# Dense neighbour sums: every fp32 product as three bf16 products

## The reference

```python
def _fa_layer(h, row, col, Wt_l, bt_l, Wg_l, bg_l):
    h = h @ Wt_l.T + bt_l
    deg = jnp.clip(jax.ops.segment_sum(ones, row, num_segments=n), 1.0)
    dinv = deg ** (-0.5)
    g = jnp.tanh(h[row] @ Wg_l + bg_l)
    norm = g * dinv[row] * dinv[col]
    msg = norm[:, None] * h[row]
    out = jax.ops.segment_sum(msg, col, num_segments=n)
    return out + h
```

## Time and profile before

| what | value |
|---|---|
| median of 3 runs | 3548.09 us (3545.02 to 3555.73) |
| profiled execution, its own time | 3552.29 us |
| its span | 3550.4 us |
| instructions in the profile | 56998 |
| PE busy | 2215.2 us, 62% |
| DVE busy | 2218.8 us, 62% |
| POOL busy | 2026.6 us, 57% |
| dense passes in the span | about 3026 to 3261 us and 3298 to 3534 us |

### The profile page before, as it was taken

The page is one execution under the profiler, slowest core; times in us unless marked ns, Lnnn a source line. Parts: engine busy times, 40 slices in busy tenths (PEclk is TensorE's granted clock), DMA queues, the critical chain, the costliest instruction groups (busy, mean ns, idle before and its releaser), DMA issues.

```text
span 3550.4 us, 56998 instructions
## 1 busy us (share of the span) xinstructions
PE 2215.2 (62%) x15272; PEld 1972.0 (56%) x15273; DVE 2218.8 (62%) x5812; ACT 1284.5 (36%) x3489; POOL 2026.6 (57%) x2076
## 2 busy tenths in 40 slices
PE   4991240566665556766556756735555555999998
PEld 3991230455554345555456656725444453998998
DVE  8997961777776645555536656575787777433434
ACT  4220020233222123333356777735777774000000
POOL 1777777777776577777357777716777770000000
PEclk9995555666666665565565565567778777999999
DMA  2210000111213222333333333325444441221222
GB/s 84 69 57 4 4 22 28 49 53 53 52 53 44 57 71 87 89 88 89 49 93 78 80 80 77 71 15 155 132 131 128 130 117 25 73 75 52 68 74 63
DMA packets 171613, 249.97 MB, mean 70 GB/s; under 512 B 52006, under 2 KB 120412, under 8 KB 171154
## 3 DMA queue, kind: packets, MB, share of 16 engines
q0 software_dynamic: 72704, 138.94, 16.7%
q1 hardware_dynamic: 94276, 96.20, 9.4%
q10 hardware_dynamic: 4430, 12.43, 1.1%
HBM read 217.00 MB, written 30.41 MB: 70 GB/s over the span
## 4 chain that ended last, share of the span: by engine, by line
POOL 47%; PE 22%; issue 17%; DVE 8%; ACT 3%; DMA 2%; DVEq 1%; POOLq 0%; ACTq 0%; SPq 0%
POOL arena L715 20%; POOL pool L715 17%; PE psum L1505 8%; POOL rec_dram L692 7%; PE psum L1501 5%; POOL ACC L715 2%; PE psum L1231 2%; PE psum L1425 2%; DVE ACC L2339 1%; ACT pool L888 1%; PE psum L1269 1%; ACT pool L816 1%; DMA arena<-tab_dram,tblk 1%; PE psum L1106 1%; DVE pool L1726 1%
## 5 line engine op out<-in xcount | busy, mean ns | idle before, releaser
L715 POOL DMA_INDIRECT arena<-tab_dram,tblk x832 | 797.5, 959 | 411.0 <-issue 250.3
L692 POOL DMA_INDIRECT rec_dram<-arena,ACC x400 | 396.3, 991 | 195.9 <-issue 119.1
L715 POOL DMA_INDIRECT pool<-tab_dram,arena x416 | 402.6, 968 | 131.9 <-issue 126.5
L1552 PE MATMUL psum<-pool 128*128 128x136 f32 (+1 forms) x1664 | 362.0, 399 | 81.0 <-DVE pool L2263 74.8
L1552 PEld LDWEIGHTS psum<-pool 128*128 128x128 f32 x1664 | 335.6, 290 | 92.7 <-issue 51.3
L1383 PE MATMUL psum<-pool 128*128 128x128 f32 x832 | 193.1, 426 | 301.1 <-DMA pool<-tab_dram,arena 228.1
L2119 DVE CAST pool<-pool 128x1024 f32<-128x1024 uint8 x264 | 182.3, 694 | 278.4 <-PE psum L1505 168.2
L1383 PEld LDWEIGHTS psum<-pool 128*128 128x128 f32 x832 | 180.0, 328 | 305.5 <-DVE pool L2132 134.6
L715 POOL DMA_INDIRECT pool<-tab_dram,tblk x272 | 276.2, 1015 | 125.9 <-issue 79.9
L857 ACT ACTIVATE arena<-psum,key 128x128 bf16<-128x128 f32 x416 | 146.4, 377 | 479.1 <-PE psum L1326 479.1
L1505 PE MATMUL psum<-arena,pool 128*128 128x128 f32 x2504 | 300.2, 277 | 0.0
(11 more groups left out here) (373 smaller groups left out, 4923.8 us busy)
## 6 DMA issues: line engine op xcount, KB each, us to landing
pool<-items_dram SPq DMA_DIRECT2D x264, 128.0 KB, 2.0
pool<-dst_dram SPq DMA_DIRECT2D x104, 256.0 KB, 3.5
items_dram<-pool SPq DMA_DIRECT2D x132, 128.0 KB, 1.7
arena<-tab_dram,tblk POOLq DMA_INDIRECT x832
HN<-in_edge_attr_dram ACTq DMA_DIRECT2D x23, 500.0 KB
pool<-tab_dram,arena POOLq DMA_INDIRECT x416
rec_dram<-arena,ACC POOLq DMA_INDIRECT x400, 2.1
pool<-tab_dram,tblk POOLq DMA_INDIRECT x272
```

Source lines behind the costliest of these rows:

```text
L692: nc.gpsimd.indirect_dma_start(rec_dram, bass.IndirectOffsetOnAxis(ap=row_all[:, c:c + 1], axis=0), rec_all[:, c, :], None).then_inc(s_sca ...
L715: nc.gpsimd.indirect_dma_start(to[:, j, :], None, tab_dram[k], bass.IndirectOffsetOnAxis(ap=idx[:, G * g + j:G * g + j + 1], axis=0)).then ...
L1552: last_ = nc.tensor.matmul(bank[j // 3][:, (j % 3) * ww:(j % 3 + 1) * ww], OHF[:, half, j, :], weighed[k][:, half, j, :], start=True, stop ...
```

## The change

In the dense passes every product with an fp32 item and the fp32 table becomes three products, with the item in bf16 (counts, exact) and with three bf16 parts of the table that add up to the fp32 value. The first part is the upper half of each fp32 number, read in place with a step of two bf16 elements (`high`). The remainder goes to `rest`, what is then left to `tail`, both fp32 and both read by their upper halves too. DVE makes `rest` and `tail` for each chunk as the table is written. The registers of a pack of later items are loaded right behind the last product of the pack of later items before it, where they were loaded right ahead of their own pack.

```diff
+        bite16 = [b[:, 0:PACK * P // 2].bitcast(BF16) for b in bite32]
+        rest = big[:, NP:2 * NP]
+        tail = arena[:, 3 * NB * D + NB * 8:3 * NB * D + NB * 8 + NP]
+        def high(ap):
+
+            halves = ap.bitcast(BF16)
+            (step, count) = halves.ap[-1]
+            return bass.AP(halves.tensor, halves.offset + 1, [*halves.ap[:-1], [2 * step, count // 2]])
...
+                ahead = item_regs(0)
                 for m, b in bites(k):
-                    vals = item_regs(b - firsts) if b >= firsts else None
+                    vals = ahead if b >= firsts else None
                     pe.wait_ge(s_cast, m + 1)
                     for j in range(PACK):
-                        item, w = bite32[m % HELD][:, P * j:P * (j + 1)], PACK * b + j
+                        item, w = bite16[m % HELD][:, P * j:P * (j + 1)], PACK * b + j
                         if vals:
-                            last = nc.tensor.matmul(psum[:, bass.ds(vals[G + j] * P, P)], item, table[:, bass.ds(vals[j] * AW, D)],
-                                                    start=False, stop=False)
+                            to = psum[:, bass.ds(vals[G + j] * P, P)]
+                            for of in (high(table[:, bass.ds(vals[j] * AW, D)]), high(rest[:, bass.ds(vals[j] * D, D)]),
+                                       high(tail[:, bass.ds(vals[j] * D, D)])):
+                                last = nc.tensor.matmul(to, item, of, start=False, stop=False)
                         elif j == 0 or w < NB * NB:
                             d, of = min(w, NB * NB - 1) // NB, min(w, NB * NB - 1) % NB
-                            last = nc.tensor.matmul(psum[:, d * P:(d + 1) * P], item, table[:, of * AW:of * AW + D], start=False, stop=False)
+                            for part in (table[:, of * AW:of * AW + D], rest[:, of * D:(of + 1) * D], tail[:, of * D:(of + 1) * D]):
+                                last = nc.tensor.matmul(psum[:, d * P:(d + 1) * P], item, high(part), start=False, stop=False)
                     last.then_inc(s_part, 1)
+                    if vals and b + 1 < PACKS:
+                        ahead = item_regs(b + 1 - firsts)
...
                     dve.wait_ge(s_taken, before(stage, c, MADE) + 1)
+                    whole = TAB[:, 4 * c:4 * c + n, 0:D]
+                    link(v.tensor_tensor(feature_chunk(rest, c, n), whole, high(whole), ALU.subtract))
+                    link(v.tensor_tensor(feature_chunk(tail, c, n), feature_chunk(rest, c, n), high(feature_chunk(rest, c, n)), ALU.subtract))
                     dve.sem_inc(s_table, 1)
...
-                    v.tensor_copy(bite32[m % HELD], bite8[m % LONG]).then_inc(s_cast, 1)
+                    v.tensor_copy(bite16[m % HELD], bite8[m % LONG]).then_inc(s_cast, 1)
```

## The result

| | before | after |
|---|---|---|
| median of the runs shown side by side | 3547.64 us (4 runs) | 3837.50 us (4 runs, 3832.84 to 3851.16) |
| ratio after / before, 95% interval | | 1.081 [1.0789, 1.083] |
| profiled execution, its own time | 3552.29 us | 3851.16 us |
| its span | 3550.4 us | 3849.4 us |
| first dense pass | 3026.0 to 3261.0, 235.0 us | 3035.3 to 3406.5, 371.2 us |

The change makes the kernel slower by 8.1%; the forecast was 3822 us, that is 7.7%. The span grows by 299.0 us, and nearly all of it is in the two stretches that the change edits: 136.2 + 149.4 = 285.6 us in the passes, 9.3 ahead of the first one, 4.1 between them. A pass is taken from the start of PE's first product to the start of its last one, which for the kernel before is 0.2 us less than in the prediction.

What follows compares the result with a forecast made beforehand. The PE sequencer bounds the passes: load 1.16 + first items 1.67 + addresses 4.24 = 7.07 us a round; two passes +265 us, subtractions +9, giving 3822 us. Main case (65%) 3720 to 3930; 8 in 10, 3650 to 3960 us.

Steps and rivals of the forecast that it cites:

- Address price of an item, 0.53 us: Dense passes, later items: sequencer time for one item's three products at register addresses, 0.25 + 0.14 + 0.14 us.
- The load, 1.16 us: Dense passes: each of 52 register loads a pass stops the sequencer from issuing for 1.16 us, 60 us a pass.
- Why the load is exposed: Dense passes: moved behind later items, the load meets an empty queue; before, about 16 queued fp32 pairs (1.79 us) hid it.
- First items, 1.67 us a round at a middle clock: Dense passes: 20.9 products a round beyond the 16 queued are exposed, at 0.08 us each.
- PE's busy share, about a half: Sign in the dense passes: PE, full before, would be busy only about half of the time.
- Idle time put down to "issue": Sign in the dense passes: the profile would ascribe PE's idle time to issue, over a microsecond around each load.
- Clock well under 0.99: Sign in the dense passes: granted TensorE clock falls; the forecast took in 3772 us all at 2.4 GHz, 3881 at 1.2.
- Subtractions, +9 us (3 and 6): DVE's two subtractions a chunk as tables are written: 3 us exposed in the first table, 6 in the second.
- The cast, at nothing: DVE's cast of items to bf16 in the dense passes: at most 0.69 us in rounds of 7 us, costing nothing.
- Hidden loads: Rival, 12%: in the passes register loads stay hidden and only addresses bind, a round of 5.91 us, 3701 us.
- array-bound pass: Rival, 10%: the array bounds the passes, register arithmetic and loads vanish beneath the queue, 3453 us, faster.
- "Both addresses each time": Rival, 10%: every product of a later item works out both addresses, 0.75 us an item, 8.83 us a round, 4004 us.

Runs made afterwards that it cites:

- e1: Changed kernel with the second and third product of later items reading rest and tail at a constant address: 3548.69 us, ratio to before 1.0002.
- e3: Changed kernel with the registers loaded once a pass, so all packs of later items use the first pack's blocks: 3455.24 us, ratio to before 0.974.
- e10: Changed kernel with register loads of 32 numbers instead of 16 in 51 of 52 packs a pass: 3979.22 us, ratio to before 1.1194.
- e2: Changed kernel with the register load put back ahead of its own pack, behind first items: 3857.43 us, ratio to before 1.0874.
- e5: Changed kernel with only first items split into bf16, later items one fp32 product, loads ahead of their own pack: 3567.86 us, ratio to before 1.006.
- e6: Changed kernel with only first items split into bf16, later items one fp32 product, loads a pack ahead: 3538.50 us, ratio to before 0.9966.
- e8: As e5, with block numbers multiplied beforehand on DVE, one fused register instruction an item: 3532.48 us, ratio to before 0.9951.
- e8b: As e6, with block numbers multiplied beforehand on DVE, one fused register instruction an item: 3503.89 us, ratio to before 0.9874.
- e4: Changed kernel without DVE's two subtractions a chunk: 3834.56 us, ratio to before 1.0809.

## Why the prediction was right, and where it was not

- **The verdict and its reason: right.** Slower, because the PE sequencer and not the array sets a pass. e1, e3 and e10 each show it: half of the register instructions less and the loss is gone; none at all and PE is full at 182 us; 105 us more of loads and 103.0 us more of idle time. In the profiled execution, whose sum was 3826, the 3851 us hold 20 us more in the passes than forecast and 4 outside them.
- **Address price of an item, 0.53 us:** 0.583 us measured, a tenth more. The count was right: 0.25 + 0.14 + 0.14 stands for two instructions and one and one, and there are four, so the psum address is indeed worked out once. The price of each was low. e1, where two are left, has 0.27 us for them in place of the 0.25 of rows 4, and the other two take 0.31 us in place of the 0.28 from L1337's rows. 416 x 0.053 = 22 us a pass.
- **The load, 1.16 us: right**, 1.105 us by its row and 1.01 us of idle time for 1.03 us of width (e10).
- **Why the load is exposed: wrong.** "What hides it now is the queue", "it now does so when nothing covers it": I blamed the new place. The load is exposed in either place once three bf16 products an item leave the queue empty (e2: 381 and 386 us against 371 and 385). The forecast was right since it counted the load in full, but the cure that I would have drawn from it, putting the load back, is worth nothing or less. The place counts only where an item at register addresses keeps the array about as long as the sequencer, or longer (e5 to e6, e8 to e8b: 29 us each).
- **First items, 1.67 us a round at a middle clock:** 1.32 and 1.58 us. The 16 pairs held ready were near: in 102 of the 104 rounds 17 of the first items' products had not started when the first register instruction behind them did. The cost of 0.08 us a product came close; the first pass had more of the high clock than I gave it. I had this term too high and the one for the items too low, and they offset each other: 7.07 us a round forecast, 7.14 and 7.40 measured. That the sum came so near is in part luck. At a depth of 64 instructions, as the Trainium skill has it ("TensorE: Matmul & The Clock Gate", "Part 1: The HAM clock gate (the "warmup" mystery)"), the term would have been 8.6 products, 0.5 to 0.9 us, which neither pass shows.
- **PE's busy share, about a half: wrong.** 85% in both windows. A record lasts from 0.22 us to 0.31 us while the products follow each other in 0.057 to 0.107 us, so three products in 0.6 us look like 0.4 us of work. The idle time of the groups and the granted clock told more than the share.
- **Idle time put down to "issue": wrong in name**, as the first part shows; the place and length are as forecast, about 1 us around each load.
- **Clock well under 0.99: right.** What I set aside as lying within the forecast is a cost in its own right: e1 got it back, e10 lost more of it.
- **Subtractions, +9 us (3 and 6): right** in sum, 3.5 and 4.5 us by e4. The beginning of the first pass moved by 9.3 us in all. 1.2 us of it came from above (the first chunk is written at 3013.73, before it was 3012.54), 3.5 from the subtractions and 3.3 from the lower clock while the table was made (e4). The 1.3 us left are the clock too, in the seven products that clear psum ahead of the pass (1.52 us before, 2.84 after). I had counted on PE's products ahead of the pass being left as they are; they were, but their clock was not. The first register load (3032.6 to 3033.7) now stands ahead of the first product, but beneath these seven, and costs nothing.
- **The cast, at nothing: right.** 88 us of DVE a pass, and each pack cast long before its turn.
- **Rivals.** Hidden loads and an array-bound pass are ruled out for this kernel by e10 and the windows; the second came true in e3, within 3 us of what it had been worked out at. "Both addresses each time" would have been six instructions an item; there are four. One slip in the numbers: the lower end of my own range, 3720, goes with 0.41 us an item at the middle clock; at the high clock, which the range was said to take in, it is 3672.

What is left open: the exact share of the lower clock in the 299 us. It was not varied by itself. An estimate from the first items alone, whose 1.32 and 1.58 us a round would be 1.19 us at 2.4 GHz, is (0.13 + 0.39) x 52 = 27 us in the two passes; against the 1.07 us that e1 had left at the high clock it is 40 us.

## What to carry to other kernels

Where addresses come from registers, count the sequencer's instructions before the array's columns: splitting a product into cheaper ones multiplies the address work. In this kernel each register instruction took the sequencer 0.13 to 0.15 us, and a bf16 product gives the array 0.058 us of work, so the array waits as soon as what is queued ahead has run out. Split the products at constant addresses, keep those at register addresses large, and do multiplications of indices beforehand on an idle engine. An experiment that doubles a suspected cost priced it cleanly where moving it said nothing; and idle time ascribed to an engine that itself waits for the idle one belongs to neither.

## What the runs showed of the hardware

- A fused register instruction is recorded with 74 ns (median), but the next one starts 129 to 153 ns after it (L1514).
- When the sequencer comes to the first register instruction behind a pack of first items, 17 of their products have not started, in 102 of 104 rounds (L1518, L1514).
- Loads of registers grow with their width, 0.593 us for 8 numbers, 1.105 for 16, 2.132 for 32, and 1.03 us more of load in each of 102 rounds left PE 103.0 us more of idle time (e10).
- bf16 products of 128 columns went on at 0.058 us each over 3126 of them, with new weights for each and with every second element read (e3).
- The granted clock was 0.99 in e3 (PE busy 181.87 of 181.90 us) and in e1 (190.40 of 229.30 us), 0.85 and 0.81 in the changed kernel, 0.76 and 0.74 in e10, where PE's idle time ahead of first items is twice as long.
